# Maxima over the keys by square block transposes on VectorE, in a Flamingo block on one core

## The reference

```
xn = layernorm(ctx) * gm + bm ; ln = layernorm(layernorm(x)) * gl + bl
q = ln @ Wq ; k, v = split([xn ; ln] @ Wkv)            # 974 keys, 8 heads of 64
sim = (q * 8) @ k.T                                    # per head, 224 x 974
sim = sim - max over the keys
x = x + tanh(g_xattn) * (softmax(sim) @ v) @ Wout
h = relu(layernorm(x) @ W_fc.T) ** 2 ; y = h @ W_proj.T   # width 2048
x = x + tanh(g_ffn) * (spikes of y over 5 steps) / 5
```

## Time and profile before

| | |
|---|---|
| median of 3 runs | 1070.77 us (1070.26 to 1070.95) |
| the profiled execution | 1070.37 us |
| its span, first to last instruction | 1068.5 us |
| mean granted TensorE clock | 0.999 of full speed |
| TensorE busy (matmul) | 1048.5 us, 98% |
| VectorE busy | 747.2 us, 70% |
| ScalarE busy | 592.7 us, 55% |
| GpSimd busy | 307.4 us, 29% |

### The profile page before, as it was taken

One profiled execution on the slowest core, in us unless ns is written; L12 is line 12 of the kernel. 1 busy time (PEld: TensorE's weight loads), 2 busy tenths in 40 slices (PEclk: granted clock), 3 DMA queues, 4 the chain that ended last, 5 costly groups with the idle time before them and its releaser, 6 DMA issues.

```text
span 1068.5 us, 19370 instructions
## 1 busy us (share of the span) xinstructions
PE 1048.5 (98%) x7105; PEld 862.6 (81%) x7105; DVE 747.2 (70%) x1166; ACT 592.7 (55%) x1147; POOL 307.4 (29%) x284
## 2 busy tenths in 40 slices
PE   5999999999999999999999999999999999999997
PEld 5878778877887877887788788787788888998886
DVE  7378877867877787686796778759535555485766
ACT  5558447655655754765574576457446433445535
POOL 4333634335434353433444434343000000000000
PEclk9999999999999999999999999999999999999999
DMA  6302010101201101010120200013431000300111
GB/s 193 133 1 76 2 35 20 54 0 34 75 0 34 67 8 34 11 64 0 34 75 0 74 0 0 26 36 103 145 102 46 12 1 20 100 1 25 36 59 40
DMA packets 31891, 47.43 MB, mean 44 GB/s; under 512 B 2284, under 2 KB 11516, under 8 KB 31852
## 3 DMA queue, kind: packets, MB, share of 16 engines
q1 hardware_dynamic: 31716, 46.74, 13.6%
q10 hardware_dynamic: 136, 0.17, 0.1%
HBM read 39.56 MB, written 7.34 MB: 44 GB/s over the span
## 4 chain that ended last, share of the span: by engine, by line
PE 95%; DVE 3%; DMA 1%; issue 0%; SPq 0%; ACT 0%; DVEq 0%
PE work L477 41%; PE work L641 14%; PE score L654 13%; PE heads_out L593 9%; PE score L556 9%; PE score L492 2%; PE maxes L578 1%; PE maxes L568 1%; PE heads_out L605 1%; PE score L841 1%; DMA xin<-in_ctx 1%; PE heads_out L477 1%; DVE on L1403 0%; PE maxes L477 0%; PE work L624 0%
## 5 line engine op out<-in xcount | busy, mean ns | idle before, releaser
L1823 POOL TENSOR_TENSOR dsum<-dsum,probs 125x448 f32<-125x448 f32 x186 | 226.0, 1215 | 14.6
L477 PE MATMUL work<-wv,xT 128*125 128x512 f32 (+1 forms) x768 | 187.4, 398 | 0.0
L477 PE MATMUL work<-xT,wk 128*128 128x486 f32 (+2 forms) x768 | 183.9, 390 | 0.5 <-DVE kst L1368 0.5
L477 PEld LDWEIGHTS work<-wv,xT 128*125 128x125 f32 (+1 forms) x768 | 137.8, 183 | 36.7 <-issue 2.3
L641 PE MATMUL work<-zT,wf 128*128 128x512 f32 (+1 forms) x768 | 164.3, 364 | 0.1
L477 PEld LDWEIGHTS work<-xT,wk 128*128 128x128 f32 x768 | 140.2, 188 | 29.9 <-issue 4.6
L961 ACT ACTIVATE probs<-score 125x448 f32<-125x448 f32 (+1 forms) x256 | 119.9, 549 | 72.1 <-PE score L556 71.8
L641 PEld LDWEIGHTS work<-zT,wf 128*128 128x128 f32 x768 | 131.4, 189 | 23.1 <-issue 0.8
L1820 POOL TENSOR_TENSOR dsum<-probs 125x448 f32<-125x448 f32 x31 | 35.7, 1152 | 391.0 <-ACT probs L967 391.0
L1356 DVE TENSOR_TENSOR probs<-probs,maxes 125x1792 f32<-125x1792 f32 x64 | 128.2, 2014 | 5.7 <-PE maxes L578 5.2
L654 PE MATMUL score<-hT,wp 128*128 128x512 f32 (+1 forms) x576 | 117.4, 354 | 0.0
(11 more groups left out here) (190 smaller groups left out, 1424.9 us busy)
## 6 DMA issues: line engine op xcount, KB each, us to landing
xin<-in_ctx SPq DMA_DIRECT2D x42, 250.0 KB
neuron<-in_L_ffn_W_fc SPq DMA_DIRECT2D x16, 256.0 KB, 4.5
neuron<-in_L_ffn_W_proj SPq DMA_DIRECT2D x16, 256.0 KB, 2.8
xres<-in_x SPq DMA_DIRECT2D x16, 224.0 KB, 2.6
x_scratch<-xres SPq DMA_DIRECT2D x16, 224.0 KB, 2.4
xin<-in_x SPq DMA_DIRECT2D x14, 224.0 KB, 9.3
zt<-x_scratch SPq DMA_DIRECT2D x3, 1024.0 KB, 6.4
fin<-x_scratch SPq DMA_DIRECT2D x3, 1024.0 KB, 5.6
```

Source lines behind the costliest of these rows:

```text
L477: mm = pe.matmul(bank, lhs(i, k), rhs(j, k), start=(n == 0), stop=(n == len(passes) * chunks - 1))
L1823: pool.tensor_tensor(total[0:ROWS[t]], total[0:ROWS[t]], tile(t), ALU.add).then_inc(dchain if t < TILES - 1 else dsum_done, 1)
```

## The change

Per pair, `maxima` makes one instruction over both heads and all 128 partitions, writes its square blocks (32 by 32) turned over into `maxes` with VectorE's `transpose`, and reduces each block's 32 columns: `rmax`, 128 by 14, holds for each of 14 blocks of 32 queries and each of four groups of 32 partitions a column of maxima. TensorE transposes `rmax` once (14 by 128), VectorE reduces over the four groups and writes the result four times side by side into `qmax`, TensorE transposes `qmax` once (128 by 128), and VectorE's `transpose` of the 14 columns, each repeated 32 times, gives the row of maxima on all partitions, now in `mx` in SBUF, from which `subtract` reads it. `max_transposes` no longer waits for `sub_done`. The partitions of `top` from 96 up are filled once with the lowest number, by GpSimd ahead of its fill of `probs`; the rows of `qmax` beyond 14 are filled with zero once. `rmax` takes the place of `qmax` among the tensors that are kept, and `qmax` moves into space of `spare2`.

```diff
--- before.py
+++ after.py
@@ -33,6 +33,8 @@
     HALF = (KEYS // 2 + 1) // 2 * 2
     XO = 2
     PAIRS = HEADS // 2
+    SQ = 32
+    QB = 2 * L // SQ
     QSCALE = float(DH) ** 0.5
     VOFF = 96
     HP = P // 2
@@ -83,7 +85,7 @@
         ve = sb(keep, "ve", [P, TILES])
         rstd = sb(keep, "rstd", [P, TILES])
         tick = sb(keep, "tick", [P, 3])
-        qmax = sb(keep, "qmax", [P, 4])
+        rmax = sb(keep, "rmax", [P, QB])
         eps = sb(keep, "eps", [P, 3])
         nmu = sb(keep, "nmu", [P, TILES])
         nmr = sb(keep, "nmr", [P, TILES])
@@ -109,7 +111,8 @@
         kst = sb(a, "kst", [P, 2, 2, KEYS], F32R)
         qst = sb(a, "qst", [P, 2, 2, L], F32R)
         vrow = sb(a, "vrow", [P, D])
-        sb(a, "spare2", [P, 4 * L - D - 16 * XO])
+        sb(a, "spare2", [P, 4 * L - D - 16 * XO - P])
+        qmax = sb(a, "qmax", [P, P])
         top = sb(a, "top", [P, 2, 2 * L])
         vals = sb(a, "vals", [P, TILES, D])
         probs = sb(a, "probs", [P, 4, TILES * L])
@@ -260,6 +263,9 @@
         s_copied = sem("s_copied")
         top_done = sem("top_done")
         mx_done = sem("mx_done")
+        mxs_done = sem("mxs_done")
+        rmax_done = sem("rmax_done")
+        mrow_done = sem("mrow_done")
         mxT_mm = sem("mxT_mm")
         qmax_done = sem("qmax_done")
         mxb_mm = sem("mxb_mm")
@@ -560,24 +566,13 @@
 
             def max_transposes(b, p):
 
-                pe.wait_ge(sub_done, b * HEADS + 2 * p)
-                for e in range(2):
-                    pe.wait_ge(mx_done, b * HEADS + (2 * p + e + 1))
-                    for i in range(2):
-                        at = (2 * e + i) * P
-                        mm = pe.transpose(maxes[0:LT, at:at + CT], mx[0:CT, e, i * LT:(i + 1) * LT],
-                                          ident[0:CT, 0:CT])
-                mm.then_inc(mxT_mm, 1)
+                pe.wait_ge(rmax_done, b * PAIRS + (p + 1))
+                pe.transpose(maxes[0:QB, 0:P], rmax[:, :], ident[:, :]).then_inc(mxT_mm, 1)
 
             def max_rows(b, p):
 
                 pe.wait_ge(qmax_done, b * PAIRS + (p + 1))
-                for e in range(2):
-                    for i in range(2):
-                        n = 2 * e + i
-                        mm = pe.transpose(maxes[0:CT, n * LT:(n + 1) * LT],
-                                          qmax[0:LT, n:n + 1].to_broadcast([LT, CT]), ident[0:LT, 0:LT])
-                mm.then_inc(mxb_mm, 1)
+                pe.transpose(maxes[:, 3 * P:4 * P], qmax[:, :], ident[:, :]).then_inc(mxb_mm, 1)
 
             def attend(b, p, bank=heads_out):
 
@@ -1237,7 +1232,7 @@
             kq_hi_parts(0, 0, 1, 2, first=True)
             split_hi(2, wv, 0, 1, 2, 3)
             kq_hi_parts(0, 1, 1, first=True)
-            act.wait_ge(pad_ready, 1)
+            act.wait_ge(pad_ready, 2)
             copy_scores(0, 0, 0, 1, first=True)
             kq_hi_parts(0, 1, 2, first=True)
             copy_scores(0, 0, 2, 3, first=True)
@@ -1335,24 +1330,37 @@
 
             def maxima(b, p):
 
-                n = (b * PAIRS + p) * FOLDS
-                for e in range(2):
-                    dve.wait_ge(top_done, n + (5 + e))
-                    dve.tensor_tensor(mx[0:CT, e, :], top[0:CT, e, 0:L], top[0:CT, e, L:2 * L],
-                                      ALU.max).then_inc(mx_done, 1)
+                n = b * PAIRS + p
+                squares = maxes[:, 0:2 * L]
+                dve.wait_ge(top_done, n * FOLDS + FOLDS)
+                dve.tensor_tensor(mx[:, :, :], top[:, :, 0:L], top[:, :, L:2 * L], ALU.max).then_inc(mx_done, 1)
+                dve.wait_ge(mx_done, n + 1)
+                dve.transpose(squares, mx[:, :, :].rearrange("p e l -> p (e l)")).then_inc(mxs_done, 1)
+                dve.wait_ge(mxs_done, n + 1)
+                dve.tensor_reduce(rmax[:, :], squares.rearrange("p (j a) -> p j a", a=SQ), AX.X,
+                                  ALU.max).then_inc(rmax_done, 1)
 
             def query_maxima(b, p):
 
                 dve.wait_ge(mxT_mm, b * PAIRS + (p + 1))
-                dve.tensor_reduce(qmax[0:LT, :], maxes[0:LT, :].rearrange("p (j r) -> p j r", r=P)[:, :, 0:CT],
-                                  AX.X, ALU.max).then_inc(qmax_done, 1)
+                four = maxes[0:QB, 0:P].rearrange("p (o i a) -> p o a i", o=1, a=SQ).to_broadcast([QB, P // SQ, SQ, P // SQ])
+                dve.tensor_reduce(qmax[0:QB, :].rearrange("p (o a) -> p o a", a=SQ), four, AX.X,
+                                  ALU.max).then_inc(qmax_done, 1)
+
+            def row_maxima(b, p):
+
+                dve.wait_ge(mxb_mm, b * PAIRS + (p + 1))
+                row = maxes[:, 3 * P:3 * P + QB].rearrange("p (j o) -> p j o", o=1).to_broadcast([P, QB, SQ])
+                dve.transpose(mx[:, :, :].rearrange("p e (j a) -> p (e j) a", a=SQ), row).then_inc(mrow_done, 1)
 
             def subtract(b, h):
 
-                dve.wait_ge(mxb_mm, b * PAIRS + (h // 2 + 1))
+                if h % 2 == 0:
+                    row_maxima(b, h // 2)
+                    dve.wait_ge(mrow_done, b * PAIRS + (h // 2 + 1))
                 e = h % 2
                 v = probs[0:CT, h % 4, :].rearrange("p (t l) -> p t l", t=TILES)
-                row = maxes[0:CT, e * L:(e + 1) * L].rearrange("p (o l) -> p o l", o=1)
+                row = mx[0:CT, e, :].rearrange("p (o l) -> p o l", o=1)
                 dve.tensor_tensor(v, v, row.to_broadcast([CT, TILES, L]), ALU.subtract).then_inc(sub_done, 1)
 
             def kq_lo_parts(b, c, *us, first=False):
@@ -1606,6 +1614,7 @@
             dve.memset(ones[:, :], 1.0).then_inc(const_ready, 1)
             dve.memset(halfneg[:, :], -0.5).then_inc(const_ready, 1)
             dve.memset(mv[:, :, :], 1.0).then_inc(const_ready, 1)
+            dve.memset(qmax[:, :], 0.0)
             dve.memset(eps[:, 0:1], EPS)
             dve.memset(eps[:, 2:3], -THRESHOLD)
             dve.memset(eps[:, 1:2], EPS * EPS).then_inc(const_ready, 1)
@@ -1855,8 +1864,10 @@
                 pool.affine_select(out=m[:, :], in_=m[:, :], compare_op=ALU.not_equal, fill=1.0, base=0,
                                    pattern=[[-1, P]], channel_multiplier=1).then_inc(ident_ready, 1)
             pool.wait_ge(ident_ready, 4)
+            pool.memset(top[CT // 32 * 32:P, :, :], LOWEST).then_inc(pad_ready, 1)
+            pool.wait_ge(pad_ready, 1)
             pool.memset(probs[64:P, :, CTX_TILES * L:], LOWEST).then_inc(pad_ready, 1)
-            pool.wait_ge(pad_ready, 1)
+            pool.wait_ge(pad_ready, 2)
             pool.wait_ge(const_ready, 4)
 
 
```

## The result

The changed kernel takes 1060.35 us (median of 4 runs, 1059.19 to 1062.61) beside 1070.86 us for the kernel before on the same chip: a ratio of 0.9908, 95% interval 0.9895 to 0.992. That is 10.5 us faster, in the stated range and 5.4 us above the forecast of 1055. The profiled execution took 1059.53 us with a span of 1057.7 us.

The account below looks back on a forecast made before the run. TensorE was taken to bound the attention loop. -18.5 + 0.4 + 1.0 + 1.2 = -15.9 us against the profiled 1070.37 gave 1054.5, with 0.4 for the median 1054.9, rounded to 1055.0 us; range 1050 to 1065.

Parts of the forecast that it names:

- TensorE's term: Loop, TensorE: transposes fall from 3.75 to 1.20 us a batch, 0.64 us saved a pair, 18.5 us over 29 pairs.
- The rival in which lone transposes cost as much as four: TensorE is not relieved: 0.4 us for each group stays, ending between 1066 and 1072 us; chance 0.05.
- VectorE's prices: VectorE per pair: square transpose and reduction 0.65 us each, row transpose 0.65, other steps unchanged; 1.9 us more.
- The rival of slow squares: VectorE's square transposes take several cycles per element and VectorE becomes the bound; 1087 us at 2.5 us each; chance 0.10.
- So I count no stall in the loop: Loop: three places with little room for VectorE's added work were checked, and no TensorE wait was added.
- The room of 0.9 us at the gated residual: Pair 1, gated_residual(b, 1): 0.9 us stay before the value product that waits for it, with 1.25 us more work ahead.
- The room at the low parts of pair 2: Pair 2, max_rows to the product needing the low part: 0.4 us of room stay after the 0.65 us row transpose.
- The start ... Nothing: Ahead of the loop: the fills of `top` and `qmax` lie in existing waits and cost nothing; without that cover 1 us.
- The head of the last batch: At max_transposes(b, 1), TensorE waits 1.05 us for VectorE's three steps and saves 0.64: +0.4 us.
- The last batch's other two terms: VectorE's added work ahead of the last pair's subtract, +1.0 us; its two subtracts waiting for GpSimd's sums, +1.2 us.
- the second rival: VectorE gives part back in the loop: transposes and reductions about 0.5 us longer each, 1059 to 1066 us; chance 0.20.
- Its sign: In the profile after, a new TensorE wait each batch, for low parts or for a gated residual.

Follow-up runs that it names:

- The move of the residual: The changed kernel with gated_residual(b, 1) right behind pair 1's maximum, ahead of its square transpose and reduction: 1059.26 us, a batch of 87.14 us.
- the move: The changed kernel with pair (0, 0)'s maxima behind the low parts of kq_lo_parts(0, 2, 0) ahead of the loop: 1058.58 us.
- three moves of single steps: The changed kernel with kq_lo_parts ahead of the first maxima, gated_residual behind pair 1's maximum, and the last batch's pair 1 TensorE transposes one value product later: 1054.75 us.

## Why the prediction was right, and where it was off

- **TensorE's term was right.** 8 x 0.107 + 0.34 = 1.20 us a batch was forecast for the new transposes; the chain has 1.13. Here their number and not their size sets the price: a transpose with 14 columns as weights and one with 128 both take 0.11 us. The rival in which lone transposes cost as much as four is out.
- **VectorE's prices were right but for the maximum.** Square transposes 0.66 and 0.64 us (forecast 0.62), reduction 0.625, the reduction in short rows 0.675 like the one before (0.678). The estimate from the Trainium skill (VectorE: DVE Perf Modes, The three transpose paths) was 0.64 us. The rival of slow squares is out. The advice of the Trainium skill (VectorE: DVE Perf Modes, Rules for kernel authors) to leave a 128 x 128 transpose that may land in PSUM to TensorE fits the kernel before, which is 10.5 us slower here. The maximum was taken as an instruction of 0.62 us; it takes 1.05 us in the mean. The two that it replaces took 0.585 us each, so in sum VectorE spends less than forecast, 74.91 us a batch and not 76; but where it is long it is what is missing from the forecast.
- **"So I count no stall in the loop" failed**, by 0.2 us a batch. With the 1.13 us that the transposes take, 2.62 us should have been saved and 2.34 were: 0.28 are missing. The room of 0.9 us at the gated residual was worked out with 0.69 us for the two maxima, which is what they took at this place, and beside GpSimd's sums: these started at 240.80 us, the maxima at 240.92. In the changed kernel the sums start at 237.59 us and the maximum at 237.82, and it takes 1.40 us, while six sums take 7.57 us and not 7.97. I read it so that a sum waited before and VectorE waits now; the prediction says that VectorE waits, but not that the wait can change sides. What decides it no run shows. The move of the residual gave the 0.2 us back; the last 0.08 us I can't place. The room at the low parts of pair 2 held: the row transpose ended in time, 193.59 + 0.84 = 194.43 against a product at 193.64 + 1.33 = 194.97.
- **"The start ... Nothing" failed**, by 2.4 us, or 2.6 counted from the first product of keys: the largest single miss. Only the two fills were costed, and the pairs ahead of the loop were counted among the 29 that save. VectorE's list there has a different order, with the maxima ahead of a low part that TensorE needs (1.06 us, shown by the move) and the statistics ahead of the reduction (1.0 us, seen as a wait, not cured). Some 0.5 us remain: the product behind the second wait takes 3.01 us in place of 2.77, and the rest is open. The fills themselves were hidden: the root behind GpSimd's starts at 7.05 us, and at 7.00 before.
- **The head of the last batch was mis-sized.** Forecast 1.05 us of wait, measured 2.01: once more a maximum of 1.40 us in place of 0.65, for the rest some 0.2 us, as the maximum started 0.79 us ahead of TensorE's arrival and not 0.91, and at the hand-overs.
- **The last batch's other two terms were right in sum and off each**: +1.0 and +1.2 against 2.5 together, in part by luck. Up to the first subtract of the last pair the stretch grew by 0.6 us and not 1.0, from there on by 1.85 and not 1.2. With one operand in PSUM 1.5 us of it go, net. The forecast had counted half a sum for each subtract, and not that the sums, themselves held up by 3.6 us, reach into VectorE's next instruction. The rule of the Trainium skill that it rested on (SBUF — State Buffer, Who interferes with whom) agrees with the trace: the subtracts of 2.54 and 2.97 us with two SBUF operands, and 2.0 us with a PSUM operand.
- The time came out where the second rival had placed it, 1059 to 1066, and in part by its mechanism. Its condition did not come true: no square transpose and no reduction was 0.5 us longer than forecast. Its sign did: the gated residual holds TensorE up in each batch, by 0.2 us and not by 0.5 to 1.2. What VectorE gives back, it gives back at single places in the order and in the last batch. The prediction gave 1050 to 1059 a chance of 0.65, and 1059 to 1066 one of 0.20.

## What to carry to other kernels

When work moves from a full engine to one with spare time, the spare time of the whole doesn't count; go through every place where the full engine waits for the other, with the durations that will hold at that place (here the maximum beside GpSimd's sums took 0.69 us before and 1.40 us after), and go through the lists ahead of and behind the loop as closely as the loop. An operand's place in memory is part of its cost: PSUM or SBUF for a second operand decided 1.5 us without changing an element of the result. And once such a change is in, its losses can be taken back by order alone: three moves of single steps gave 4.6 us by the stretches and 5.9 by the medians, beside the 10.5 us of the change.

## What the runs showed of the hardware

- VectorE's square transpose of 128 x 448 4-byte elements takes 0.660 us from SBUF to PSUM and 0.62 to 0.65 us from PSUM to SBUF, the latter with a column repeated 32 times as its input: close to an elementwise instruction of that size (0.61 to 0.63 us, line 1333 of the kernel before).
- The wait between VectorE and GpSimd goes both ways: beside subtracts with two SBUF operands, at 2.54 and 2.97 us, six GpSimd sums took 11.23 us, beside those with one operand in PSUM, at 2.0 us, 7.66 us.
- A TensorE transpose with 14 weight columns is no cheaper in the chain than one with 128; repeated, each cost 0.108 us.
- TensorE's granted clock can fall near the start of this kernel: in two of the twelve profiles it was 0.50 of full speed from 21 to 23 us, after TensorE had stood still for 1.57 and 1.47 us ahead of 18.8 us, waiting for its input; in the ten others it was 1.00 from 20 to 25 us. The same 36 products took 9.03 and 9.14 us in place of 8.02.
